# Second scan, first two batches: y summed by accumulating DMA; the low half of each shared unit on GpSimd

## What is computed

```
x = x + scan0(ctx) * silu(layernorm(x))      # scan0: 512 channels, 16 states, length 512
x = x + moe(layernorm(x))                    # 16 routed experts (top 4) and a shared expert
x = x + scan1(ctx) * silu(layernorm(x))
x = x + ternary_ffn(layernorm(x))            # weights rounded to -1, 0, 1
```

```
h_n[t] = exp(delta[t] * A_n) * h_n[t-1] + delta[t] * u[t] * B_n[t]
y[t]   = sum over n of h_n[t] * C_n[t]  +  D * u[t]
```

## Time and profile before

| | |
|---|---|
| median of 3 runs | 2080.75 us (2074.3 to 2083.68) |
| profiled execution, its own time | 2079.93 us |
| its span in the profile | 2077.8 us |
| DVE busy | 1727.8 us, 83% |
| PE busy | 1617.4 us, 78% |
| POOL busy | 1329.9 us, 64% |
| ACT busy | 1182.9 us, 57% |
| L540, adds to y on POOL | 128 x 2366 ns, half of them in slots 10 to 83 |
| L1796, low part on DVE | 88 x 418 ns |
| mean DMA rate over the span | 149 GB/s |

### The profile page before, as it was taken

How to read it: one execution, slowest core, us unless ns; L and a number is a source line. 1 busy time by engine, 2 the same in 40 slices (tenths; PEclk the granted TensorE clock), 3 DMA queues, 4 the chain that set the end, 5 groups by cost and what they waited for, 6 DMA issues and landing times. The chain is left out here.

```text
span 2077.8 us, 26814 instructions
## 1 busy us (share of the span) xinstructions
PE 1617.4 (78%) x8322; PEld 916.6 (44%) x8322; DVE 1727.8 (83%) x2277; ACT 1182.9 (57%) x1820; POOL 1329.9 (64%) x641
## 2 busy tenths in 40 slices
PE   4675765765673968888888898999989998167888
PEld 1222322222222635656566655666646565033444
DVE  3999999999996586999699958888668787788886
ACT  5676776775743326656766555445454454246675
POOL 2689888888992001998099926888438887764120
PEclk7787988988996789999999999999999999579999
DMA  6646546456536522442333254555535632732100
GB/s 212 230 162 221 203 169 225 164 171 198 179 108 219 201 91 88 142 127 87 128 117 107 85 196 143 189 187 181 180 132 187 233 123 97 222 102 80 40 21 26
DMA packets 129716, 310.35 MB, mean 149 GB/s; under 512 B 23824, under 2 KB 33168, under 8 KB 124464
## 3 DMA queue, kind: packets, MB, share of 16 engines
q1 hardware_dynamic: 86496, 208.37, 29.6%
q10 hardware_dynamic: 31232, 60.17, 8.2%
q0 software_dynamic: 11856, 40.12, 6.5%
HBM read 217.12 MB, written 91.49 MB: 149 GB/s over the span
## 5 line engine op out<-in xcount | busy, mean ns | idle before, releaser
L550 POOL TENSOR_TENSOR ssm_hs<-ssm_hs,ssm_Cs 128x1024 f32<-128x1024 f32 x128 | 314.3, 2465 | 90.7 <-DVE ssm_hs L517 90.7
L550 POOL TENSOR_TENSOR moe_hs<-moe_hs,moe_Cs 128x1024 f32<-128x1024 f32 x128 | 302.0, 2359 | 51.9 <-DVE moe_hs L517 50.8
L517 DVE TENSOR_TENSOR_SCAN moe_hs<-moe_dA,moe_bu 128x1024 f32<-128x1024 f32 x128 | 292.6, 2286 | 21.4 <-ACT moe_dA L431 12.9
L540 POOL TENSOR_TENSOR moe_U<-moe_U,moe_hs 128x1024 f32<-128x1024 f32 x128 | 302.8, 2366 | 6.4
L1599 PE MATMUL moe_pgu<-all_Wreg,moe_xt 128*128 x1896 | 302.6, 314 | 0.0
L517 DVE TENSOR_TENSOR_SCAN ssm_hs<-ssm_dA,ssm_bu 128x1024 f32<-128x1024 f32 x128 | 291.7, 2279 | 0.1
L347 PE MATMUL ssm_pY<-ssm_hs,ssm_ident 128*128 128x512 f32 x512 | 275.2, 665 | 5.9 <-POOL ssm_hs L550 5.9
L1549 PE MATMUL moe_pgu<-all_Wreg 128*128 128x256 f16 x2112 | 253.4, 278 | 22.8 <-DVE moe_hsl L1796 18.0
L1549 PEld LDWEIGHTS moe_pgu<-all_Wreg 128*128 128x128 f16 x2112 | 209.7, 100 | 69.5 <-DVE moe_hsl L1796 16.6
L1599 PEld LDWEIGHTS moe_pgu<-all_Wreg,moe_xt 128*128 128x128 f16 x1896 | 186.0, 98 | 93.5
L834 POOL TENSOR_TENSOR ssm_wlo<-ssm_wst,ssm_whi 128x1360 f16<-128x1360 f32 (+2 forms) x63 | 188.4, 2991 | 33.8 <-ACT ssm_wst L751 33.8
(11 more groups left out here) (288 smaller groups left out, 3131.2 us busy)
## 6 DMA issues: line engine op xcount, KB each, us to landing
ssm_wst<-in_w_all SPq DMA_DIRECT2D x51, 680.0 KB, 5.2
y_d<-moe_yo ACTq DMA_DIRECT2D x79, 256.0 KB
all_Wreg<-w_hi SPq DMA_DIRECT2D x16, 1088.0 KB
all_Wreg<-w_lo SPq DMA_DIRECT2D x16, 1088.0 KB
w_hi<-ssm_whi SPq DMA_DIRECT2D x51, 340.0 KB, 2.3
w_lo<-ssm_wlo SPq DMA_DIRECT2D x51, 340.0 KB, 3.1
ssm_Cs<-c_d SPq DMA_DIRECT2D x64, 256.0 KB, 5.5
moe_Cs<-c_d ACTq DMA_DIRECT2D x64, 256.0 KB, 4.3
```

The lines of the kernel that those rows point to most:

```text
L517: self.nc.vector.tensor_tensor_scan(self.hs[:, j, :, :].rearrange("p k t -> p (k t)"), self.dA[:, q, :, :].rearrange("p k t -> p (k t)"), ...
L540: self.nc.gpsimd.tensor_tensor(Y, Y, self.hs[:, j, :, :], ALU.add).then_inc(self.acc_done, 1)
L550: self.nc.gpsimd.tensor_tensor(self.hs[:, j, :, :], self.hs[:, j, :, :], self.Cs[:, i:i + 1, :].to_broadcast([P, HC, L]), ALU.mult)\
```

## The change

For the steps of batches 0 and 1 (s below BYDMA = 64) POOL no longer adds `hs` to `U`. It issues a DMA that adds it in place, SBUF to SBUF, 128 x 1024 fp32. The DMAs of the two halves of the channels have a semaphore each, and a DMA waits for the one before it on the same half (step s - 2). The scan waits for the add of four steps before, as it did, now on those semaphores, and not at all in the first four steps. Batches 2 and 3 keep the add on POOL.

The low part of each shared unit moves from DVE to POOL, which stands behind the scan's DMA and ahead of the scan's multiply there. POOL can't read PSUM, so the second silu instruction now writes to a new SBUF buffer `hu` (one buffer, 128 x 256 fp32, laid over the routed experts' `hth` and `htl`), and ACT's high part reads it there too. The silu instruction therefore waits for the low part of the unit before. `sh_up(u)` needs only the silu of unit u - 2 to free its PSUM bank, no longer its low part.

```diff
+BYDMA = 2 * STEPS
...
+    def wait_added(self, eng, s):
+
+        if s < BYDMA:
+            eng.wait_ge(self.acc_in[s % 2], 16 * (s // 2 + 1))
+        else:
+            eng.wait_ge(self.acc_done, s - BYDMA + 1)
...
     def pool_add(self, pool, b, half, s, j):
         Y = self.U[:, b % self.dbl, half * HC:(half + 1) * HC, :]
         pool.wait_ge(self.prod_done, s + 1 + R)
-        pool.wait_ge(self.acc_done, s + R)
-        self.nc.gpsimd.tensor_tensor(Y, Y, self.hs[:, j, :, :], ALU.add).then_inc(self.acc_done, 1)
+        if s >= 2:
+            self.wait_added(pool, s - 2)
+        if s < BYDMA:
+            pool.dma_start(Y, self.hs[:, j, :, :], accum_op=ALU.add).then_inc(self.acc_in[half], 16)
+        else:
+            self.nc.gpsimd.tensor_tensor(Y, Y, self.hs[:, j, :, :], ALU.add).then_inc(self.acc_done, 1)
...
@@ POOL
+                def sh_low(u):
+                    pool.wait_ge(s_hi, u + 1)
+                    if u >= 3:
+                        pool.wait_ge(s_dn, u - 2)
+                    nc.gpsimd.tensor_tensor(hsl[:, u % 3, :], hu, hsh[:, u % 3, :], ALU.subtract).then_inc(s_lo, 1)
...
+                    if g <= 0 and slot:
+                        sh_low(slot - 1)
...
@@ PE, sh_up
                     if u >= 2:
-                        pe.wait_ge(s_lo, u - 1)
+                        pe.wait_ge(s_hh, u - 1)
...
@@ ACT, sh_high
-                    nc.scalar.copy(hsh[:, u % 3, :], pgu[u % 2][:, TS:2 * TS]).then_inc(s_hi, 1)
+                    nc.scalar.copy(hsh[:, u % 3, :], hu).then_inc(s_hi, 1)
...
@@ DVE, sh_silu_up
-                    nc.vector.scalar_tensor_tensor(out=u_, in0=u_, scalar=0.5 * HS / (XS * WS) ** 2, in1=s_,
+                    if u:
+                        dve.wait_ge(s_lo, u)
+                    nc.vector.scalar_tensor_tensor(out=hu, in0=u_, scalar=0.5 * HS / (XS * WS) ** 2, in1=s_,
                                                    op0=ALU.mult, op1=ALU.mult).then_inc(s_hh, 1)
-
-                def sh_low(u):
-                    dve.wait_ge(s_hi, u + 1)
-                    nc.vector.tensor_tensor(hsl[:, u % 3, :], pgu[u % 2][:, TS:2 * TS], hsh[:, u % 3, :],
-                                            ALU.subtract).then_inc(s_lo, 1)
```

More of the change, by code:

```diff
@@ L244, in __init__ @@
         self.prod_done = m.sem("prod_done")
+        self.acc_in = [m.sem(f"acc_in{h}") for h in range(2)]
         self.acc_done = m.sem("acc_done")
@@ L281, in store_y @@
         else:
-            sp.wait_ge(self.acc_done, (b + 1) * STEPS + R)
+            for h in range(2):
+                self.wait_added(sp, (b + 1) * STEPS - 2 + h)
         sp.dma_start(y_ssm[b * L:(b + 1) * L, :].rearrange("(k p) n -> p k n", p=P),
@@ L368, in act_conv @@
             if not self.alone:
-                act.wait_ge(self.acc_done, b * STEPS + R - 3 + c // 2)
+                self.wait_added(act, b * STEPS - 4 + c // 2)
         self.nc.scalar.activation(self.acc[:, c, :], self.conv_in(b, c), ACT.Identity,
@@ L513, in dve_scan @@
         q = j % self.ring
-        dve.wait_ge(self.sum_done if self.alone else self.acc_done, s + 1)
+        if self.alone:
+            dve.wait_ge(self.sum_done, s + 1)
+        elif s >= R:
+            self.wait_added(dve, s - R)
         dve.wait_ge(self.exp_rdy, s + 1)
@@ L524, in pool_start @@
         pool.sem_inc(self.prod_done, R)
-        if not self.alone:
-            pool.sem_inc(self.acc_done, R)
     def pool_y_init(self, pool, b):
@@ L1378, in experts_and_ssm @@
         xth, xtl = xt[:, 0, :, :, :], xt[:, 1, :, :, :]
-        hth = m.sb("hth", [P, 3, P], F16)
-        htl = m.sb("htl", [P, 3, P], F16)
+        ht = m.sb("ht", [P, 2, 3 * P], F16)
+        hth, htl = [ht[:, k, :].rearrange("p (q n) -> p q n", q=3) for k in range(2)]
+        hu = ht[:].rearrange("p k n -> p (k n)")[:, 0:2 * TS].bitcast(F32)
         yo = m.sb("yo", [P, 2, H])
@@ L1513, in _ @@
                     b, at = entry(slot)
-                    if at is None or at < PRO:
-                        continue
-                    s, half, n = step(b, at)
-                    if at == PRO:
-                        S.pool_y_init(pool, b)
-                    else:
-                        S.pool_add(pool, b, 1 - half, s - 1, (s - 1) % R)
+                    s, half, n = step(b, at) if at is not None and at >= PRO else (None, None, None)
+                    if s is not None:
+                        if at == PRO:
+                            S.pool_y_init(pool, b)
+                        else:
+                            S.pool_add(pool, b, 1 - half, s - 1, (s - 1) % R)
+                    if g <= 0 and slot:
+                        sh_low(slot - 1)
+                    if s is None:
+                        continue
                     S.pool_step(pool, s, s % R)
@@ L1838, in _ @@
                         S.dve_bu(dve, b, half, s)
-                    if g <= 0 and slot:
-                        sh_low(slot - 1)
                     if s is not None:
```

## The result

The changed kernel takes 2087.78 us in the median of 13 runs (2085.02 to 2092.54), the kernel before 2079.89 (2074.3 to 2083.85, 13 runs). The ratio is 1.0043, with a 95% interval of 1.003 to 1.0055: 7.9 us slower, where 7.5 us faster was forecast. The range (2063 to 2094) and the class "within 0.5%" hold it, the sign is wrong. The profiled execution took 2089.63 us (span 2087.8), 9.7 more than that of before.

A forecast was written before the change was run, and what follows sets the result against it. ACT's loop of scan, silu, high part and decays was taken to bound the 4.79 us slot. Gains 1.9 + 2.0 + 0.7 + 1.3 + 2.5 - 0.9 = 7.5 us gave a forecast of 2073 us, range 2063 to 2094.

The forecast's parts named there:

- within 0.5%: Whole kernel: a time that can't be told from no change, 0.5% being 10.4 us; chance 0.46.
- Nothing behind the shared stage should give it back: After the shared stage: its last slot leads into routed slots waiting for weights, so the 7.5 us gain stays.
- part 4: POOL's new work in a slot: issue 1.0 us, low part 0.66, hidden; delays at batch ends and last unit cost 0.9.
- What bounds the slot: Ordinary step slot: ACT's loop of scan, silu, high part and two decays, 4.79 us; full POOL isn't waited for.
- part 1: Low part off DVE: ordinary slots gain nothing, slots with transposition 1.9 us, with sum 2.0, delta work before batches 0.7.
- Part 2: Silu written to SBUF, high part reading it there: taken as zero, bounds -0.03 and +0.03 us a slot in 62 slots.
- Part 3: PE no longer waiting for low parts: 1.3 us off at the stage's start, 1.23 behind each of two batches, 2.5.
- one of the prediction's own signs of being wrong: In the shared units: the prediction is wrong if L1820 waits for POOL.
- Part 5: Adding DMAs: landing taken as 6 us, bounds 3.7 and 7.8; traffic 240 to 350 GB/s fits under 433 seen.
- Nothing comes of it: Rival, step slots: low part arrives just in time on POOL, its waits eat the gains, 2077 to 2082 us; chance 0.12.
- the DMAs land late: Rival, step slots: landings over 9.58 us block POOL, 2116 us at 11; milder, ACT waits for weights, 2092; chance 0.10.

The follow-up runs named there:

- experiment 2: Changed kernel with the last shared unit's (87) high part moved ahead of `act_u` in ACT's program: 2079.01 us, ratio 0.9997 to the kernel before.
- 1: Changed kernel with the last two of batch 1's 32 additions done by GpSimd again: 2083.01 us, ratio 1.002 to the kernel before.
- 3: Changed kernel with additions by DMA kept, but the low part on DVE from PSUM and PE's wait as before: 2085.52 us, ratio 1.003 to the kernel before.
- experiment 5: Changed kernel with unit 87's high part ahead of `act_u` and, in step slots, decays ahead of the high part: 2067.57 us, ratio 0.9939 to the kernel before.
- experiment 10: The kernel of experiment 5 with all 64 additions of the first two batches left out (y incomplete): 2056.05 us, ratio 0.9887 to the kernel before.

## Why the prediction was wrong

**The step that failed: "Nothing behind the shared stage should give it back", and with it the 0.3 us that part 4 gave the last unit.** It looked at the routed units' weights and not at who waits for the last addition. I wrote that a DMA is waited for by its half's next one and by a scan; the third waiter, `store_y`, and behind it `act_u` and unit 87's high part, I left out, and an addition that lands 9 us after its issue began has no slack there. The end of the shared stage took 7.8 us more. Shown by experiment 2 (moving the one instruction behind it gives 8.8 us, where the kernel before gains 2 by it), 1 (two earlier additions give 4.8) and 3 (the additions alone bring the loss).

**What bounds the slot: right.** Ordinary slots hardly moved, DVE is idle 0.63 us for the decays (0.6 said), and breaking that loop in experiment 5 gave 4.32 us. DVE's own round was put at 4.19 without the low part; 4.32 is what it takes, for the reason under part 1.

**Part 1: wrong in size, 4.6 us said, 1.5 seen.** Its row counted 0.33 us a slot; it is 0.11, because bu to scan is 1.35 us without the low part between. 14 slots became shorter by 0.10 to 0.11. The two runs of delta work, 0.7 us said, lost: units 7 to 9 take 6.71 + 8.61 us instead of 6.64 + 8.20, since a multiply on DVE (L493, before L482) takes 1.63 us beside GpSimd's low part where it took 1.22, and unit 9's second silu waits 0.53 us for GpSimd.

**Part 2: the upper bound, taken as zero.** +0.03 us in an ordinary slot (0.41 against 0.37 for the high part), some 1.5 us in all, which eats part 1. 31 slots take 152.65 us against 152.85, from silu to silu. From first scan to last they take 153.14 against 152.84, with the wait behind L544 in them: the steps as a whole gained nothing.

**Part 3: right.** 1.3 us were said for the start; units 1 to 4 gain 14.65 - 13.50 = 1.15. Behind batch 0, units 40 to 46 take 21.86 instead of 23.20 us, 1.34 (1.23 said), and units 82 to 87 17.55 instead of 18.65. It came by a new wait, though: unit 41's L1820 waits 2.84 us for GpSimd's low part of unit 40, behind the last multiply, and the shorter convolutions make up for it. Those beside a low part on GpSimd take 2.60 us, not 2.31, as L493 did above: the move brought a little of the contention back. The rule of the Trainium skill on who contends in SBUF (SBUF — State Buffer, Who interferes with whom) is borne out by 2.31 us without GpSimd's addition beside the convolution, 4.28 with one and 6.01 with more; its full 1.97 us twice were not to be had.

**Part 4: right in the steps.** The issue is 0.87 us and follows the multiply by 0.30 (1.0 said). The low part takes 0.97 right behind an issue and 0.67 elsewhere (0.66 said), and 0.58 us of POOL's wait for the scan are left. L532 (now L544) delays L1820 by 0.4 us in each batch, 0.3 said. In all L1820 waits for POOL five times, 6.9 us, so one of the prediction's own signs of being wrong came true; POOL never waits for a landing. The last unit's 0.3 us was the 7.8 above.

**Part 5: the landing right, its cost too low.** 6.0 us in the median (6 said), but 4.5 to 10.2, and 11.4 for the store behind it, with the expert weights ahead of it; the 3.2 us that the Trainium skill's fit (DMA: Bandwidth & Descriptors, Anatomy of one DMA) gave were not reached once. I compared a rate (231 GB/s) with the best rate seen and called it fitting. By busy share the engines were at 0.93. In this kernel that cost little beside the end; in experiment 5 it costs 10 of the 11.5 us that experiment 10 gains (8.1 in the steps and 1.8 at the end).

**Rivals.** "Nothing comes of it" describes the steps; "the DMAs land late" had the right cause in the wrong place: I priced it per slot from 9.58 us on, where it counted once, at the batch's end. In sum: 2.5 us gained in the shared units, 7.5 said, and 7.8 lost behind them. That makes 5.3; the remaining 2.6 us of the 7.9 between the medians are not placed. Experiment 2's shared units took 439.8 us, with waits for the ternary stores between the batches (units 47 to 49 take 27.9 us, before 25.3), so the 2.5 us gained may not be there in each execution; this is argued, not shown.

## What to carry to other kernels

When an operation moves from an engine to a DMA, list everyone who waits for its last instance, not only the steady state's waiters, and ask what stands behind each of them in its engine's program: here one instruction behind a wait cost more than all slots gained. An instruction between a producer and its consumer on one engine is worth only what it adds to the wait that is there anyway. And first find the loop that sets the slot: reordering two ACT instructions gave the kernel before 9 us, while relieving two nearly full engines gave none. And a late instance can cost more than its lateness: here the store slipped by a few microseconds and got behind 2.2 MB of loads, and TensorE came out of the wait at half its clock.
